# The last scan steps and the hand-over to expert 0: last products cut and moved, counts and sends reordered, last rows multiplied in high and low parts

## What is computed

```
dA = jnp.exp(d_t[..., None] * A)
state = state * dA + (d_t * u_t)[..., None] * B_t[:, None, :]
y_t = jnp.einsum('ben,bn->be', state, C_t)
```

```
probs = jax.nn.softmax(xr @ Wg, axis=-1)
gate_vals, expert_idx = jax.lax.top_k(probs, K)
h = jax.nn.relu(jnp.einsum('ecd,edf->ecf', dispatched, w1))
expert_out = jnp.einsum('ecf,efd->ecd', h, w2)
```

## Time and profile before

| what | value |
|---|---|
| median of 3 runs | 302.5 us (301.12, 302.5, 307.67) |
| the profiled execution's own time | 300.18 us |
| its span in the trace | 298.4 us |
| mean granted TensorE clock | 0.878 |
| TensorE busy | 252.1 us (84%) |
| VectorE busy | 219.0 us (73%) |
| ScalarE busy | 175.5 us (59%) |
| GpSimd busy | 220.4 us (74%) |
| chain that ended last, TensorE's share | 47% |

### The profile page before, as it was taken

The page is one execution under the profiler, slowest core; times in us unless marked ns, Lnnn a source line. Parts: engine busy times, 40 slices in busy tenths (PEclk is TensorE's granted clock), DMA queues, the critical chain, the costliest instruction groups (busy, mean ns, idle before and its releaser), DMA issues.

```text
span 298.4 us, 4932 instructions
## 1 busy us (share of the span) xinstructions
PE 252.1 (84%) x1508; PEld 223.5 (75%) x1508; DVE 219.0 (73%) x381; ACT 175.5 (59%) x384; POOL 220.4 (74%) x180
## 2 busy tenths in 40 slices
PE   8959777857867587894979999999999999999950
PEld 7748555546745475683967999999999999999940
DVE  3899998999999999999652556667584848484610
ACT  2798766967995775577052566364747465564410
POOL 1799599869959999999716836868585868777552
PEclk9996997897979855576687999999999999999995
DMA  6579610080005431051161354563636464644111
GB/s 166 212 248 313 228 64 0 5 315 1 0 1 196 162 114 64 35 176 37 63 226 59 82 208 178 174 210 136 220 117 209 137 214 159 219 173 175 34 46 36
DMA packets 15073, 40.38 MB, mean 135 GB/s; under 512 B 2922, under 2 KB 9900, under 8 KB 12112
## 3 DMA queue, kind: packets, MB, share of 16 engines
q1 hardware_dynamic: 11792, 33.15, 33.0%
q0 software_dynamic: 2816, 6.32, 6.1%
q10 hardware_dynamic: 448, 0.70, 0.9%
HBM read 32.72 MB, written 8.49 MB: 138 GB/s over the span
## 4 chain that ended last, share of the span: by engine, by line
PE 47%; POOL 5%; DVE 5%; issue 4%; DMA 2%; POOLq 1%; ACT 0%; SPq 0%
PE ps L983 13%; PE ps L985 13%; PE ps L984 13%; DVE h L1186 3%; POOL expert_rows L387 2%; PE ps L992 2%; PE ps L1001 2%; DVE hc L1197 1%; PE ps L1074 1%; POOL dbu L342 1%; POOL w1lo L417 1%; PE ps L966 1%; DMA xe<-expert_rows 1%; DMA expert_rows<-xrow,sloti 1%; PE ps L810 1%
## 5 line engine op out<-in xcount | busy, mean ns | idle before, releaser
L1186 DVE TENSOR_TENSOR_SCAN h<-ps,dbu 128x512 f32<-128x512 f32 x64 | 74.6, 1207 | 2.0 <-ACT ps L536 1.9
L342 POOL TENSOR_TENSOR dbu<-du,bsb 128x1024 f32<-128x1024 f32 x31 | 72.7, 2364 | 0.7 <-DMA bsb<-b_rows 0.4
L536 ACT ACTIVATE ps<-delta,anegs 128x255 f32<-128x255 f32 x128 | 53.3, 462 | 9.5 <-DVE h L1186 6.9
L1358 DVE SCALAR_TENSOR_TENSOR htlo<-ps,hthi 128x320 fp32r<-128x320 f32 x64 | 30.4, 487 | 35.0 <-ACT hthi L690 35.0
L429 POOL TENSOR_TENSOR w2lo<-w2raw,w2hi 128x512 fp32r<-128x512 f32 x30 | 38.3, 1305 | 12.0 <-ACT w2hi L681 11.9
L791 PE MATMUL ps<-stack,sels 64*128 64x256 f32 x64 | 19.3, 390 | 32.2 <-DVE hc L1197 29.0
L810 PE MATMUL ps<-cst,hc 128*128 128x128 f32 x256 | 46.4, 341 | 0.0
L791 PEld LDWEIGHTS ps<-stack,sels 64*128 64x128 f32 x64 | 12.3, 238 | 41.5 <-issue 41.4
L810 PEld LDWEIGHTS ps<-cst,hc 128*128 128x128 f32 x256 | 37.6, 176 | 4.5 <-issue 2.2
L983 PE MATMUL ps<-xthi,w1hi 128*128 (+1 forms) x128 | 40.5, 317 | 0.0
L983 PE MATMUL ps<-hthi,w2hi 128*128 128x320 f32 x128 | 40.3, 315 | 0.0
(11 more groups left out here) (154 smaller groups left out, 465.1 us busy)
## 6 DMA issues: line engine op xcount, KB each, us to landing
w1raw<-in_w SPq DMA_DIRECT2D x8, 1024.0 KB, 4.8
w2raw<-in_w SPq DMA_DIRECT2D x8, 1024.0 KB, 4.9
bsb<-b_rows SPq DMA_DIRECT2D x7, 1024.0 KB, 7.2
expert_rows<-fill SPq DMA_DIRECT2D x1, 2580.0 KB, 15.9
xe<-expert_rows SPq DMA_DIRECT2D x8, 258.0 KB, 5.5
out<-x SPq DMA_DIRECT2D x4, 256.0 KB, 5.2
xnat<-in_x SPq DMA_DIRECT2D x1, 768.0 KB, 7.3
xe<-expert_rows SPq DMA_DIRECT2D x8, 64.5 KB, 5.6
```

What stands on the lines that cost most here:

```text
L342: nc.gpsimd.tensor_tensor(dbu[j % DRING][:], du[:, :, None, cols(b)].to_broadcast([P, EC, 2, L]), bsb[b % 2][:, None, 2 * p:2 * p + 2, :]. ...
L536: ins = nc.scalar.activation(decays(g % SLOTS_DA)[:, c, i * L + 1:(i + 1) * L], delta[:, c, b * L + 1:(b + 1) * L], ACT.Exp, scale=anegs[: ...
L1186: nc.vector.tensor_tensor_scan(h[g % HRING][:, c].rearrange("p n t -> p (n t)"), decays(g % SLOTS_DA)[:, c, :], dbu[g % DRING][:, c].rearr ...
L1358: nc.vector.scalar_tensor_tensor(out=htlo[:, f, :], in0=ps[:, f % 4, 0:CAP], scalar=0.0, in1=hthi[:, f, :].bitcast(F32), op0=ALU.max, op1= ...
```

## The change

- **Last C:** the C of step 31 is cast together with that of step 30, ahead of the state sum of step 29.
- **Last product:** `mult` of step 31 is cut into the two halves of the channels; `add_state` takes the channel halves one after the other, with a wait for each.
- **Counts:** for the last batch they stand ahead of both `place_rows`, with 4 more `keep_clock` products before them.
- **Last rows:** ScalarE writes the normalised rows once, casts them to float32r (`rowhi`), and writes the second copies after the exponentials; VectorE makes `rowlo` after `takes`. TensorE multiplies both parts with `takes`, now float32r, high parts of both chunks first.
- **GpSimd:** the sends of batch 2 stand ahead of the four low parts of w1.
- **Expert 0:** expert 1's rows are loaded ahead of the small loads `meta0` and turned at f == 5 instead of 4; half of the split of w1 for expert 1 stands ahead of its rows' split, `metas(0)` behind it; the first fetch waits for `meta_done` 4 instead of 2.

The diff, without the list of semaphore names:

```diff
--- before.py
+++ after.py
@@ -145,7 +145,9 @@
         xrow = sb("xrow", [P, TILES, TOPK, ROW])
         meta0 = sb("meta0", [P, ET, 2])
         numbers = sb("numbers", [P, CAP])
-        takes = sb("takes", [P, BT, CAP])
+        takes = sb("takes", [P, BT, CAP], F32R)
+        rowhi = sb("rowhi", [P, BT, DM], F32R)
+        rowlo = sb("rowlo", [P, BT, DM], F32R)
 
         scan_mem = ExitStack()
 
@@ -275,18 +277,18 @@
             for e in range(1, NE):
                 if e == 1:
 
+                    sp.wait_ge(s["xet_psum"], KC)
                     sp.wait_ge(s["scattered1"], 16 * BT * TOPK)
+                    rows_in(1)
                     sp.dma_start(meta0[:, 0:2, :], xe_dram[0:2 * P, DM:ROW].rearrange("(t p) r -> p t r", p=P)
                                  ).then_inc(s["meta_in"], 16)
                     sp.dma_start(meta0[0:EROWS[2], 2, :], xe_dram[2 * P:CAP, DM:ROW]
                                  ).then_inc(s["meta_in"], 16)
 
-                sp.wait_ge(s["xet_psum"], e - 1 + KC)
                 if e > 1:
+                    sp.wait_ge(s["xet_psum"], e - 1 + KC)
                     sp.wait_ge(s["meta_done"], 2 * e)
-                rows_in(e)
-
-                if e > 1:
+                    rows_in(e)
                     sp.wait_ge(s["h_psum"], FC * (e - 1) + W1_LATER)
                     w1_load(e)
                 sp.wait_ge(s["w2hi_done"], WP * e)
@@ -411,13 +413,13 @@
                 if b == 3 and p in (2, 3):
                     send(p)
                 drive(j)
+            for j in tiles_range(B - 2):
+                send(j)
             for m in range(WP):
                 fs = slice(m * FP * P, (m + 1) * FP * P)
                 pool.wait_ge(s["w1hi_done"], m + 1)
                 nc.gpsimd.tensor_tensor(w1lo[:, :, fs], w1raw[:, :, fs], w1hi[:, :, fs].bitcast(F32),
                                         ALU.subtract).then_inc(s["w1lo_done"], 1)
-            for j in tiles_range(B - 2):
-                send(j)
             row_rstd(B - 1)
             pool.wait_ge(s["xe_in"], 32)
             for j in tiles_range(B - 1):
@@ -431,7 +433,7 @@
 
             def fetch(e):
 
-                pool.wait_ge(s["meta_done"], 2 * (e + 1))
+                pool.wait_ge(s["meta_done"], 2 * (e + 1 if e else 2))
                 if e >= 1:
 
                     pool.wait_ge(s["res_out"], 16 * ET * e)
@@ -669,9 +671,18 @@
 
             x1_turned(B - 1)
             row_scales(B - 1)
-            for j in range((B - 1) * BT, TILES):
-                normalise(j)
+            act.wait_ge(s["ln_scale"], B)
+            for j in tiles_range(B - 1):
+                nc.scalar.activation(xrow[:, j, 0, 0:DM], x1[:, j, :], ACT.Identity,
+                                     bias=nmx[:, j:j + 1], scale=rx[:, j:j + 1]).then_inc(s["row_done"], 1)
+            for t in range(BT):
+                act.wait_ge(s["row_done"], t + 1)
+                nc.scalar.activation(rowhi[:, t, :], xrow[:, (B - 1) * BT + t, 0, 0:DM], ACT.Copy
+                                     ).then_inc(s["rowhi_done"], 1)
             top_exp(B - 1)
+            for j in tiles_range(B - 1):
+                nc.scalar.activation(xrow[:, j, 1, 0:DM], x1[:, j, :], ACT.Identity,
+                                     bias=nmx[:, j:j + 1], scale=rx[:, j:j + 1]).then_inc(s["xn_done"], 1)
             weigh(B - 1)
 
             def split_w2(e, m):
@@ -695,8 +706,10 @@
                     if f < WP:
                         split_w2(e, f)
                 if not last:
+                    for m in range(FP if first else 0):
+                        split_w1(1, m)
                     rows_hi(e + 1)
-                    for m in range(WP):
+                    for m in range(FP if first else 0, WP):
                         split_w1(e + 1, m)
                 if last:
                     for c in range(KC):
@@ -802,10 +815,13 @@
                                                skip_group_check=True)
                 ins.then_inc(s["opened"], 1)
 
-            def add_state(g, tiles):
-                pe.wait_ge(s["mult_done"], g + 1)
-                for t in tiles:
-                    for c in range(EC):
+            def add_state(g):
+                for c in range(EC):
+                    if g == STEPS - 1 and c == 0:
+                        pe.wait_ge(s["mult_half"], 1)
+                    else:
+                        pe.wait_ge(s["mult_done"], g + 1)
+                    for t in range(BT):
                         for i in range(2):
                             ins = nc.tensor.matmul(y[:, t, c * P:(c + 1) * P],
                                                    hc[g % SUMS][:, c, i, t * P:(t + 1) * P], ident, start=False,
@@ -906,15 +922,17 @@
                         logits(b - 1)
                     if p == (4 if b == B - 1 else 6):
                         counts(b - 1)
-                if g + 1 < STEPS:
+                if g + 1 < STEPS - 1:
                     c_cast(g + 1)
+                if g == STEPS - 3:
+                    c_cast(STEPS - 1)
                 if p == 0:
                     if b == 0:
                         pe.wait_ge(s["u_done"], 2 * EC)
                     else:
                         pe.wait_ge(s["gate_done"], b)
                     open_sums(b)
-                add_state(g, range(BT)).then_inc(s["ysum_done"], 1)
+                add_state(g).then_inc(s["ysum_done"], 1)
 
                 if b == 0 and p == 1:
 
@@ -974,9 +992,10 @@
             turn(zst[:, tiles_of(B - 1), :], False, True).then_inc(s["xt_psum"], 1)
             keep_clock(3, DABANK)
             logits(B - 1)
+            keep_clock(4, DABANK)
+            counts(B - 1)
             pe.wait_ge(s["xe_in"], 32)
             place_rows(0)
-            counts(B - 1)
             place_rows(1)
 
             def split_mm(out_, hi_a, lo_a, hi_b, lo_b, start, stop):
@@ -1052,7 +1071,7 @@
 
                 for c in range(KC if last else 1):
                     for f in range(FC):
-                        if first and f == 4:
+                        if first and f == 5:
 
                             turn_rows(1)
                         if f % FP == 0:
@@ -1067,14 +1086,19 @@
                     ins.then_inc(s["o_psum"], 1)
 
 
+            def take(part, c, last):
+                for t in range(BT):
+                    ins = nc.tensor.matmul(ps[:, 6 + c, 0:CAP], part[:, t, c * P:(c + 1) * P], takes[:, t, :],
+                                           start=False, stop=(last and t == BT - 1), skip_group_check=True)
+                return ins
+
+            pe.wait_ge(s["takes_done"], BT)
+            pe.wait_ge(s["rowhi_done"], BT)
             for c in range(KC):
-                for t in range(BT):
-                    pe.wait_ge(s["takes_done"], t + 1)
-                    pe.wait_ge(s["xn_done"], (B - 1) * BT + t + 1)
-                    ins = nc.tensor.matmul(ps[:, 6 + c, 0:CAP], xrow[:, (B - 1) * BT + t, 0, c * P:(c + 1) * P],
-                                           takes[:, t, :], start=False, stop=(t == BT - 1),
-                                           skip_group_check=True)
-                ins.then_inc(s["xet_psum"], 1)
+                take(rowhi, c, False)
+            pe.wait_ge(s["rowlo_done"], BT)
+            for c in range(KC):
+                take(rowlo, c, True).then_inc(s["xet_psum"], 1)
             pe.wait_ge(s["slots_done"], B)
             expert(0, True, False)
             with pe.Fori(1, NE - 1) as e:
@@ -1194,10 +1218,17 @@
                 dve.wait_ge(s["c_psum"], g + 1)
                 if g >= SUMS:
                     dve.wait_ge(s["ysum_done"], g - SUMS + 1)
-                nc.vector.tensor_tensor(hc[g % SUMS][:].rearrange("p c n t -> p c (n t)"),
-                                        h[g % HRING][:].rearrange("p c n t -> p c (n t)"),
-                                        ps[:, c_bank(g):c_bank(g) + 1, :].to_broadcast([P, EC, 2 * L]),
-                                        ALU.mult).then_inc(s["mult_done"], 1)
+                if g < STEPS - 1:
+                    nc.vector.tensor_tensor(hc[g % SUMS][:].rearrange("p c n t -> p c (n t)"),
+                                            h[g % HRING][:].rearrange("p c n t -> p c (n t)"),
+                                            ps[:, c_bank(g):c_bank(g) + 1, :].to_broadcast([P, EC, 2 * L]),
+                                            ALU.mult).then_inc(s["mult_done"], 1)
+                else:
+                    for c in range(EC):
+                        nc.vector.tensor_tensor(hc[g % SUMS][:, c].rearrange("p n t -> p (n t)"),
+                                                h[g % HRING][:, c].rearrange("p n t -> p (n t)"),
+                                                ps[:, c_bank(g), :], ALU.mult
+                                                ).then_inc(s["mult_done" if c else "mult_half"], 1)
 
             def gate_y(b):
                 dve.wait_ge(s["zt_done"], b + 1)
@@ -1253,6 +1284,10 @@
```

(12 more changed lines are left out.)

4 lines of the change are left out of this document (2 added, 2 removed).

## The result

The changed kernel took 303.31 us (median of 20 runs, 301.63 to 304.16) beside 301.18 us for the kernel before on the same chip; over the rounds the ratio is 1.0049 with a 95% interval of 1.0029 to 1.0069, some 1.5 us more; small as that is, the interval leaves out 1. 302.7 us was forecast. The times of each kernel lie in two groups some 2 us apart, 14 of 20 runs in the lower one before and 5 of 20 after, and as both profiles are of the lower group, no trace here shows why fewer runs of the changed kernel fall in it. The profiled execution took 302.02 us of its own (span 300.2; before 300.18 and 298.4).

What follows compares the result with a forecast made beforehand. TensorE runs without a gap from expert 0's first product, so work ahead of it bounds the kernel. Late row turns (+2.36) and halved passes (-1.47) sum to +0.9 us: 302.7 us from 301.8, range 299.2 to 304.9.

Steps and rivals of the forecast that it cites:

- Sends ahead: GpSimd's moved w1 low parts hold VectorE's addition of x until 152.56 instead of 149.51, 3.05 us later.
- Rival A: VectorE's addition slips in between GpSimd's w1 parts, losing at most 1.3 us; expert 0 2.1 us sooner, 299.7 us; chance 0.23.
- The clock: TensorE idles some 2.5 us before the counts, its clock falls, and each half of the row turns takes 1.74 us.
- Rival B: Addition held, but TensorE's clock stays up; expert 0 in step at 160.6, 0.55 us sooner, 301.2 us; chance 0.12.
- rivals C and D: C: held, clock returns later, at 164.3, 303.8 us, chance 0.13; D: 1 us stall in expert 0 or 1, chance 0.07.
- The path from there: After the held addition: choice made at 154.6, counts, then row turns ending at 159.05, 2.36 us later than before.
- High and low parts: Last rows' product with takes: row turns' end to expert 0 in step 3.00 us instead of 4.47, counted as -1.47.
- Counts ahead of the row turns: TensorE's counts follow the choice at 154.6, key at 155.8, TensorE goes on at 155.55 with both row-turn halves.
- Last C: TensorE at the scan's end saves one change of operand, some 0.1 us, between 0 and 0.2.
- Expert 0 and after: Reordered loads, splits and fetch in experts 0 and 1 cost nothing; a missing cover would stall up to 1 us.
- The sum: Expert 0 in step: +2.36 - 1.47 = +0.9 us, the last C's 0.1 us inside its rounding.

Runs made afterwards that it cites:

- experiment 2: Kernel before with only batch 2's sends put ahead of GpSimd's low parts of w1; ratio 1.0005 to the kernel before, 301.39 us.
- experiment 4: Changed kernel with 14 instead of 4 clock products ahead of the counts; ratio 1.0006 to the kernel before, 301.89 us.
- experiment 5: Changed kernel with two of GpSimd's four low parts of w1 ahead of batch 2's sends, two behind; ratio 0.9913 to the kernel before, 299.44 us.
- experiment 6: Changed kernel with three low parts of w1 ahead of batch 2's sends, one behind; ratio 0.9881 to the kernel before, 298.53 us.
- experiment 8: experiment 6 with the counts between the row turns' halves again, without the four clock products; ratio 0.9953 to the kernel before, 300.78 us.
- experiment 9: Changed kernel with the last rows' product in float32 again, both row copies written at once; ratio 1.0053 to the kernel before, 303.41 us.
- experiment 10: Changed kernel with the last C's place, whole last product and old order of state sums back; ratio 1.0036 to the kernel before, 302.85 us.
- experiment 11: experiment 6 with the last rows' product in float32 again, both row copies written at once; ratio 0.9859 to the kernel before, 297.19 us.
- Experiment 3: Changed kernel, but VectorE's addition of x reads the gated rows from an extra PSUM copy; ratio 0.9927 to the kernel before, 299.65 us.
- experiment 12: The kernel of experiment 6 once more, in new rounds; ratio 0.9874 to the kernel before, 297.58 us.
- experiment 1: Changed kernel with GpSimd's four low parts of w1 back ahead of batch 2's sends; ratio 0.9946 to the kernel before, 299.93 us.

## Why the prediction was right, and where it was not

**The mechanism held.** *Sends ahead* were to hold the addition until 0.56 us behind the fourth w1 part, for 3.05 us. It was held for 3.26 (3.95 less 0.69), and experiments 2, 4, 5, 6, 8, 9, 10 and 11 show the same distance of 0.55 to 0.57 from one, two and four parts. Rival A (the addition slips in between) fell. Experiment 3 shows the second SBUF input as the cause.

**The clock held.** A fall behind the idle TensorE, and 1.74 us for each half of the row turns: 3.58 for both, 3.51 up to the next row. Experiment 4 shows that with the idle time filled the clock holds through the row turns, and that 1.17 us of the tail hang on it. Rival B (the clock stays up) is thus a state that 10 more unused products bring about up to the products with `takes`, but not what the change did; rivals C and D didn't come.

**The path from there was right.** The counts were to start at 154.6 and started at 155.05; of these 0.45 us most is the 0.38 by which VectorE's gate came later (all of the scan lay 0.63 later, and 0.25 were won back between step 29's product and the gate). Measured from VectorE's gate, the row turns end 11.07 us later (159.54 less 148.47), where the prediction had 10.96 (159.05 less 148.09, the gate of the old profile).

**High and low parts: the term that was mis-sized.** I had 3.00 us from the end of the row turns to expert 0 in step, where it was 4.47, and called that -1.47. It was 3.45 (159.54 to 162.99). Up to VectorE's low part the steps fit: ScalarE's high part began 2.01 us behind the row turns (2.00 forecast), `xtlo` 0.47 behind that (0.47). The 0.45 lies behind it. I had expert 0 in step 0.55 us from the start of `xtlo`, and it was 0.97: TensorE started the first product 0.26 behind the end of `xtlo`, and the row that I read for the whole 0.22 behind that. The comparison itself was also wrong. It set the new product against the old one at the clock of the old profile throughout; the old product in the same place (experiment 9) needs 3.99, because the clock comes back at 162.2, during its last passes. At full clock the traces show no saving (experiments 11 and 12). I had written that the second chunk no longer covers the turn-round, and had let it cost 0.66 us at the lower clock without asking what is left of the saving at the higher one.

**Counts ahead of the row turns: right in the sum, but not priced by itself.** The prediction put the whole +2.36 on the late choice. Experiment 2 has the same hold with the old order and loses only 0.23 us of tail. From GpSimd's last part to expert 0 in step it needs 9.43 us, and the changed order with the same float32 product (experiment 9) 10.71. By these traces it is the pair that costs: with the counts first, all of TensorE's work waits for the choice that is late. With the choice on time the same order, with its four clock products, earns about 2 us (experiment 8 against 6 and 12, with uncertainties of 2.0 and 1.5 us). No run has the counts' place changed alone in the changed kernel.

**Last C.** I took 0.1 us. The traces give 0.25, the times nothing that can be told (experiment 10). Experiment 10 also takes back the waits added to the 32 state sums, which I took at nothing, so that no run shows these by themselves. Even the 0.25 may be the clock's: the same stretch is 6.07 us in experiment 9, where the sixteen state passes ran at a higher clock, 2.09 us for 3.28.

**Expert 0 and after.** Cost at nothing, and 137.2 us from in step to the end in both kernels shows nothing. GpSimd's first fetch waited 6.33 us for the indices behind expert 1's hidden products, without holding anyone.

**The sum.** From the gate on, the two traces have +2.47 us up to the end of the row turns and -1.02 behind it; less the 0.25 of the last C that is the +1.2, where I had +0.9, and the ratio has +1.5. The level came out closer than the difference deserved, and that was luck: the 301.8 I started from lies 0.6 us above the median of 301.18 that the kernel before took beside the change.

What stays open: the 1.6 us by which experiment 1 beats the kernel before, which its trace doesn't show; what brings the clock down in one execution and not in the next; and why the scan of this profile was 0.63 us later ahead of the tail. The last is small beside what the profiles differ by at that point: the gate of the last batch starts between 147.00 (experiment 9) and 151.69 us (experiment 10), two kernels that differ little before it.

## What to carry to other kernels

Before a GpSimd tensor operation is moved, list the VectorE instructions with two SBUF inputs that lie in its new place; each waits until GpSimd's whole row of them, queued without a gap, is done, and shows that as busy time and not as idle. Fill the time in which GpSimd waits anyway (here three of four parts in 3.5 us) or give the VectorE instruction one PSUM operand, and the reordering that the hold had spoiled pays. A product that is halved in passes is worth its saving only at the clock at which it runs, and less whatever turn-round it had been hiding. Where the clock can fall, follow it to the end of the span: experiment 4 won 1.17 us ahead of expert 0 and lost 1.4 in it.

## What was not expected of the hardware

The hold reaches over instructions that are queued back to back: up to 5.11 us in experiment 9, from inside the first of four of 1.24 us each, with no slipping in at the three borders between them. The Trainium skill, SBUF — State Buffer, SBUF: two separate sides, describes an exclusive lock that is held for the whole instruction, and the other side blocks. By that alone the addition could have got in after one part, 1.2 us at most; the runs show the row of instructions held as one, and the measurement decides.

The release is the same every time: 0.55 to 0.57 us from the end of GpSimd's last part to the end of the held addition (before, in the expert loop; after; experiments 2, 4 to 6 and 8 to 11), a little less than the 0.69 that the addition takes unheld. The earlier trace rows hide how often it comes: in the trace of the kernel before, VectorE's first low part of w1 takes 2.69 or 2.70 us in all six experts of the loop, each time beside two of GpSimd's low parts of w2.

TensorE's granted clock fell behind waits of 1.13 and 1.38 us (experiments 1 and 8) as well as of 2.37, and stayed up in experiments 3, 5, 11 and 12, in 3 and 5 even behind waits of 1.99 and 2.01 us ahead of expert 0. Behind 1.98 us at the same place in experiment 6 it fell. So the length of the last wait doesn't decide it alone, and one kernel can do both (experiments 6 and 12). Whether it falls moves a single profile by 1 to 2 us, as much as the change itself, so that a single profile doesn't tell these kernels apart.
